# A two-layer macaron block on one core: the state of polynomial attention by 32x32 tiles instead of GpSimd passes, and another order of a unit's work on TensorE

## The chip, the cores and the metric

One core of one Trainium2 chip runs the whole program. The metric is device time in microseconds (us). Of the kernel before, three runs are shown; their median counts. Engines are named as in the profile: PE (TensorE; PEld its weight loads), DVE (VectorE), ACT (ScalarE), POOL (GpSimd), SP (SyncE, which issues the DMAs).

## The reference

Six sublayers follow each other on x of 4 x 1024 x 128 in float32: an MoE feed-forward, polynomial attention, the MoE again, a dense feed-forward, latent attention, the dense feed-forward again. The change touches the second one, `_L0_attn_ref`, with 16 heads of width 8:

```python
att = jnp.einsum('bhid,bhjd->bhij', q, k) * (1.0 / math.sqrt(hd))
att = jnp.where(causal[None, None], att, -jnp.inf)
lin = jnp.where((x >= -100) & (x <= 0), -0.01 * x + 1, 0.0)     # polymax(x) = (poly + lin) / 1000
poly = jnp.where(x > 0, x ** 2 + 1, 0.0)
y = jnp.einsum('bhij,bhjd->bhid', polymax(att), v)
return y.reshape(B, T, C) @ W_proj
```

## The kernel before

`attn0_phase` (from L888) works on one batch element after another. An element has 1024 tokens (8 tiles of 128) and 4 groups of 4 heads; one group of one element is a **turn** `m`, 16 in all. `pipeline` (L975) writes out the four turns of an element and loops over elements. In a turn the scores of 4 heads are made in 10 **units** k (`key_units`, L1500): for each half of the queries the diagonal tiles (units 0 and 3), two smaller units (1, 2 and 4, 5), and for the second half four full units of 128 keys by 512 queries (6 to 9). While turn m runs, the 10 **preparations** (`PREP`, L949) of turn m+1 are interleaved, one with each unit: keys k0, k1, four key/value pieces kv0 to kv3, queries q0, q1, and run0, run1.

A part of the function is linear in the score for all earlier keys, so the kernel keeps a running sum over key tiles of (key, value) products. run0 and run1 multiply keys by values on PE (L1063), DVE adds them up into `run` (L1333), and POOL makes the **state** from them by three passes over 128x1024 elements (`state`, L1003: mask and scale L1007, its low part L1011, the difference L1014). PE adds state times queries to the output (L1109), once for each half of the queries, right behind the products with `seen_one` (L1104).

Each engine runs its own queue in written order. On PE a turn is `step` (L1128): for every k the scores of unit k+1 (L1068), then preparation k (L1052, L1058 or L1063, all in the one PSUM bank `a_bank`), then for k >= 2 the values of unit k-2 (L1086), at k = 4 the small matmul `highest` (L1117) that tests the size of the scores. `values` ends a half with L1104 and L1109. ACT takes the rectified scores (L1229, or L1224 for the diagonal), then its part of the preparation (L1208 makes the low part of keys or queries, L1213 copies a kv piece), then squares (L1239), and copies the output at the end of a half (`copy_out`, L1243). DVE takes its half of the scores (`take`: L1365, or L1359 and L1361 for the diagonal), finishes keys and queries (L1315, L1320), the running sum, and the diagonal products (`diagonal`, L1372); the result of `highest` (L1348) it reads ahead of `take` of unit 6, `decide` follows at k = 6. POOL squares (L1021) and makes the state. A preparation waits until `a_bank` has been read by the one before it. At the end of a turn `correct` (L961) branches on the flag of that test; an element ends with the projection (L1182) and the residual sum.

Of the kernel before, what the change touches and what calls it, by code (L numbers as in the profile page):

```python
# [879 lines left out]
GW = 3 * P  # L880
# [7 lines left out]
def attn0_phase(nc, t, tag):  # L888


    with ExitStack() as ctx:
# [8 lines left out]
        first_rows = small[:, 3:4]  # L900
        state_mask, kv_ones, seen = small[:, 8:136], small[:, 136:392], small[:, 392:904]
        k_lift, minus_lift, half_lift = small[:, 904:905], small[:, 905:906], small[:, 906:907]
# [5 lines left out]
        KV = [sb(f"KV{q}", [P, BT, 2 * P]) for q in range(2)]  # L908
        run = sb("run", [P, BT, P])
        runm = sb("runm", [P, BT, P])  # L910
        runl = sb("runl", [P, BT, P], F32R)
        S = [sb(f"S{q}", [P, BT, P], F32R) for q in range(2)]
# [17 lines left out]
        runm_ready, runl_ready, S_ready = sem("runm_ready"), sem("runl_ready"), sem("S_ready")  # L930
# [21 lines left out]
        def width(u):  # L952

            pieces = units[u][1]
            return pieces[0][3] if len(pieces) == 1 else HALF

# [35 lines left out]
        with nc.Block() as block:  # L992
            @block.gpsimd
            def _(pool):
                for s in (runm_ready, runl_ready, S_ready, sq01_ready):
                    pool.sem_inc(s, LEAD)
                pool.memset(run[:, 0, :], 0.0).then_inc(zero_ready, 1)
                pool.wait_ge(w_in, 48)
                pool.tensor_scalar(seen_one[:, :], seen[:, 0:P], 1.0 + LIFT * LIFT, None, ALU.mult).then_inc(seen_set, 1)
                for q in range(2):  # L1000
                    pool.tensor_copy(KV[q][:, :, :], kv_ones.unsqueeze(1).to_broadcast([P, BT, 2 * P])).then_inc(kv_set, 1)

                def state(m, q):  # L1003

                    pool.wait_ge(av_ready, after(m * NU + NU - 1))
                    pool.wait_ge(y_ready, after((m - 1) * 2 - 1))
                    pool.tensor_tensor(runm[:, :, :], run[:, :, :], state_mask.unsqueeze(1).to_broadcast([P, BT, P]),  # L1007
                                       ALU.mult).then_inc(runm_ready, 1)
                    pool.wait_ge(runm_ready, after(m))
                    pool.sem_inc(pool_pause, 1)  # L1010
                    pool.tensor_tensor(runl[:, :, :], runm[:, :, :], k_low.unsqueeze(2).to_broadcast([P, BT, P]),  # L1011
                                       ALU.mult).then_inc(runl_ready, 1)
                    pool.wait_ge(runl_ready, after(m))
                    pool.tensor_tensor(S[q][:, :, :], runm[:, :, :], f32(runl[:, :, :]), ALU.subtract).then_inc(S_ready, 1)  # L1014

                def square(m, g, u):
                    n = width(u)
                    pool.wait_ge(read01, after(m * NU + u))
                    pool.sem_inc(pool_pause, 1)
                    r = R[:, slot(g % 2, u), 0:2, HALF - n:HALF]  # L1020
                    pool.tensor_tensor(r, r, r, ALU.mult).then_inc(sq01_ready, 1)  # L1021

                def step(m, g, b, more, has_next):
                    for u in OTHERS:
                        square(m, g, u)
                    if has_next:
                        state(m + 1, (g + 1) % 2)

                pipeline(pool, lambda: state(0, 0), step, lambda b, more: None)

            @block.tensor
            def _(pe):
# [3 lines left out]
                pe.wait_ge(w_low, 1)  # L1036
# [8 lines left out]
                def prepare(m, g, k):  # L1045
# [44 lines left out]
                def values(m, g, u):  # L1090
# [11 lines left out]
                    if end:  # L1102
# [25 lines left out]
                def step(m, g, b, more, has_next):  # L1128
                    for k in range(NU):
# [4 lines left out]
                        elif has_next:  # L1134
                            scores(m + 1, (g + 1) % GROUPS, 0)
                        if has_next:
# [4 lines left out]
                            if k == 5:  # L1141
# [32 lines left out]
                def finish(b, more):  # L1174
# [3 lines left out]
                    for s in range(2):  # L1178
                        for j in range(4):
                            for g in range(GROUPS):  # L1180
                                c = s * HALF + j * P
                                last = pe.matmul(e01[1][:, s, j * P:(j + 1) * P], yS[:, g, c:c + P], wp[:, g * DIM:(g + 1) * DIM],  # L1182
# [6 lines left out]
            def _(act):  # L1189
# [4 lines left out]
                act.activation(w[0][:, :, 0:P], w32[:, :, 0:P], ACT.Copy, scale=SCORE_SCALE)  # L1194
                act.activation(w[0][:, :, P:GW], w32[:, :, P:GW], ACT.Copy).then_inc(w_high, 1)
# [7 lines left out]
                def prepare(m, g, k):  # L1203
# [6 lines left out]
                    elif kind == "kv":  # L1210
                        act.wait_ge(ap_ready, after(m * NU + k))
                        act.wait_ge(y_ready, after((m - 1) * 2 - 1))
                        act.activation(KV[g % 2][:, 2 * i:2 * i + 2, :].rearrange("p j (g c) -> p (j g) c", c=ROW)[:, :, 0:3 * HD],  # L1213
                                       a_bank[:, :].rearrange("p (n c) -> p n c", c=ROW)[:, :, 0:3 * HD],
# [37 lines left out]
                def step(m, g, b, more, has_next):  # L1252
                    for k in range(NU):
                        if k + 1 < NU:
                            rectify(m, g, k + 1)
                        elif has_next:
                            rectify(m + 1, (g + 1) % GROUPS, 0)
                        if has_next:
# [5 lines left out]
                        if k == NQ0 + 1:  # L1264
                            copy_out(m, g, 0)
# [18 lines left out]
            def _(dve):  # L1284
# [5 lines left out]
                dve.wait_ge(w_high, 1)  # L1290
                dve.wait_ge(zero_ready, 1)
                dve.scalar_tensor_tensor(w[1][:, :, 0:P], w32[:, :, 0:P], SCORE_SCALE, f32(w[0][:, :, 0:P]), ALU.mult, ALU.subtract)
                dve.tensor_tensor(w[1][:, :, P:GW], w32[:, :, P:GW], f32(w[0][:, :, P:GW]), ALU.subtract).then_inc(w_low, 1)

# [13 lines left out]
                def prepare(m, g, k):  # L1308
# [13 lines left out]
                    elif kind == "run":  # L1322
                        dve.wait_ge(ap_ready, after(m * NU + k))
                        dve.wait_ge(runm_ready, after(m - 1))
                        last = 3 if i == 0 else 2
                        for h in range(last + 1):
# [6 lines left out]
                            ins = dve.tensor_tensor(run[:, c + 1, :], a_bank[:, h * P:(h + 1) * P], run[:, c, :], ALU.add)  # L1333
# [49 lines left out]
                def step(m, g, b, more, has_next):  # L1383
                    for k in range(NU):
                        if k == 5:
                            highest(m, g % 2)
# [4 lines left out]
                        if k == 6:  # L1391
# [45 lines left out]
A0_SMALL = 907  # L1437
SLOTS = 4


def attn0_weights(ctx, nc, t):

    t.attn0_w = ctx.enter_context(nc.sbuf_tensor("attn0_w", [P, GROUPS, GW], F32))
    t.attn0_wp = ctx.enter_context(nc.sbuf_tensor("attn0_wp", [P, GROUPS * DIM], F32))
# [21 lines left out]
def attn0_laid_out(np, a, r):  # L1466
    wqkv = a["L0_attn_W_attn"].reshape(DIM, 3, GROUPS, GH, HD)
    w = np.zeros((DIM, GROUPS, 3, GH, ROW), np.float32)
    for part in range(3):
        w[:, :, 0:2, :, part * HD:(part + 1) * HD] = wqkv[:, 0:2].transpose(0, 2, 1, 3, 4)  # L1470
    w[:, :, 2, :, 0:HD] = wqkv[:, 2]
    r["wqkv"] = w.reshape(P, GROUPS * GW)
    wp = np.zeros((GROUPS, GH, ROW, DIM), np.float32)
    wp[:, :, 0:HD] = a["L0_attn_W_proj"].reshape(GROUPS, GH, HD, DIM)
    r["wproj"] = wp.transpose(1, 2, 0, 3).reshape(P, GROUPS * DIM)
    row, col = np.arange(P) % ROW, np.arange(P)
    small = np.zeros((P, A0_SMALL), np.float32)
    small[:, 0] = ((row >= HD) & (row < 2 * HD)) | (row == 25)
    small[:, 1] = (row >= 2 * HD) & (row < 3 * HD)
    small[:, 2] = (row >= 24) & (row < 27)  # L1480
    small[row == 24, 904], small[row == 25, 904], small[row == 26, 904] = lift_parts(np)
    small[:, 905], small[:, 906] = -LIFT, HALF_LIFT
    small[:, 3] = row < HD
    small[:, 4:8] = np.arange(P)[:, None] // ROW == np.arange(GH)
    same = (np.arange(P)[:, None] // ROW) == (col[None, :] // ROW)
    small[:, 8:136] = same * np.where(row < 24, SLOPE, np.where(row < 26, 1.0 - HALF_LIFT * HALF_LIFT, 0.0))[:, None]
    small[:, 136:264] = ((row == 24) | (row == 25))[None, :]
    small[:, 392:904] = np.tile(np.triu(np.ones((P, P))), (1, 4))
# [699 lines left out]
```

## Time and profile before

| | us |
|---|---|
| median of 3 runs (3181.7 to 3197.34) | 3185.62 |
| the profiled execution | 3197.16 |
| its span, first to last instruction | 3195.4 |
| of it PE busy / DVE / ACT / POOL | 2832.2 / 2087.3 / 1199.9 / 836.7 |

The mean granted TensorE clock is 0.919 of full speed. The table is read with the stage in mind: these shares are averages over six sublayers with other limits, and the change touches one of them.

### The profile page before, as it was taken

Reading aid. Unit: us, or ns where it says so; the run is one execution under the profiler, and the core shown is the slowest. Engines: PE = TensorE matmul, PEld = TensorE weight load, DVE = VectorE, ACT = ScalarE, POOL = GpSimd, SP = SyncE. Lnnn points to the kernel's source line nnn. Section 1 sums busy time; section 2 is a strip of 40 time slices with the busy share of each in tenths; the row PEclk is TensorE's granted clock in tenths of the full one; section 3 lists DMA queues with packets and bytes.
Section 4 is the critical chain, followed back from the end, with each engine's and each line's share of the span. In section 5 each row is a group of like instructions: output and inputs, shape, how many; then the busy total and the mean of one; then the engine's idle time right before and its main releaser. Section 6 shows DMA issues by size and latency. Waiting matters only on the chain. (4 is left out here: it accounts for less than half of the span.)

```text
span 3195.4 us, 55424 instructions
## 1 busy us (share of the span) xinstructions
PE 2832.2 (89%) x15400; PEld 1924.1 (60%) x15400; DVE 2087.3 (65%) x5242; ACT 1199.9 (38%) x2164; POOL 836.7 (26%) x1220
## 2 busy tenths in 40 slices
PE   5999999958787888689999998869989989999986
PEld 4777777735555555467777776445465465465453
DVE  6777777747676777577777776355556556555533
ACT  2111111127565657521111111335545545545532
POOL 1222332225555555423222332001101101111100
PEclk8999999958888788899999998879999999999988
DMA  3000000000000000110000000000000000000000
GB/s 130 0 0 0 0 0 0 1 0 2 3 2 3 2 2 2 61 44 0 0 0 0 0 0 1 0 1 1 1 2 1 1 1 1 1 1 1 1 1 27
DMA packets 12996, 23.60 MB, mean 7 GB/s; under 512 B 2306, under 2 KB 7682, under 8 KB 12804
## 3 DMA queue, kind: packets, MB, share of 16 engines
q1 hardware_dynamic: 12804, 21.22, 2.0%
q8 instruction: 98, 1.61, 0.2%
q14 instruction: 94, 0.77, 0.1%
HBM read 18.52 MB, written 2.10 MB: 6 GB/s over the span
## 5 line engine op out<-in xcount | busy, mean ns | idle before, releaser
L555 DVE SCALAR_TENSOR_TENSOR moe_acc<-moe_ps,moe_comb,moe_acc 128x512 f32<-128x512 f32 x896 | 661.1, 744 | 174.5 <-PE moe_ps L304 167.9
L2017 DVE CUSTOM_DVE_ANT_0 attn_masked<-attn_psm,attn_causal 128x1024 f32<-128x1024 f32 (+7 forms) x512 | 367.6, 755 | 210.4 <-PE attn_psm L1742 199.3
L1921 ACT ACTIVATE attn_probs<-attn_pse 128x512 f32<-128x512 f32 (+1 forms) x640 | 319.9, 553 | 301.6 <-PE attn_pse L1756 301.0
L304 PE MATMUL moe_ps<-moe_Wg,moe_xh 128*128 128x512 f32 x1024 | 329.4, 403 | 25.0 <-DVE moe_Wu L501 25.0
L335 PE MATMUL moe_ps<-moe_Wd,moe_ih 128*128 128x512 f32 x1024 | 337.8, 411 | 0.0
L304 PE MATMUL moe_ps<-moe_Wu,moe_xh 128*128 128x512 f32 x1024 | 337.1, 411 | 0.0
L1772 PE MATMUL attn_psy<-attn_probs,attn_V 128*64 128x512 f32 (+3 forms) x1536 | 325.5, 524 | 0.3 <-POOL attn_probs L1677 0.3
L454 POOL TENSOR_SCALAR moe_part<-consts,moe_pick,moe_prob 128x8 f32<-128x8 f32 x256 | 98.1, 398 | 752.1 <-ACT moe_prob L389 752.1
L1677 POOL TENSOR_SCALAR_AFFINE_SELECT attn_probs<-attn_probs 128x256 f32<-128x256 f32 (+1 forms) x192 | 95.1, 495 | 757.7 <-ACT attn_probs L1921 757.7
L1021 POOL TENSOR_TENSOR attn_R<-attn_R 128x1024 f32<-128x1024 f32 (+1 forms) x128 | 215.5, 1690 | 201.6 <-DVE attn_R L1365 201.4
L1756 PE MATMUL attn_pse<-attn_qS,attn_kS 110*128 110x512 f32 (+3 forms) x768 | 233.2, 394 | 21.4 <-ACT attn_probs L1921 15.2
L304 PEld LDWEIGHTS moe_ps<-moe_Wg,moe_xh 128*128 128x128 f32 x1024 | 195.3, 192 | 73.9 <-issue 28.3
L1756 PEld LDWEIGHTS attn_pse<-attn_qS,attn_kS 110*128 110x128 f32 x768 | 120.0, 194 | 188.6 <-ACT attn_probs L1921 108.1
L388 ACT ACTIVATE moe_prob<-moe_gap 128x2 f32<-128x2 f32 x64 | 13.0, 203 | 548.4 <-DVE moe_gap L546 548.4
L335 PEld LDWEIGHTS moe_ps<-moe_Wd,moe_ih 128*128 128x128 f32 x1024 | 186.0, 191 | 41.8 <-issue 1.1
L304 PEld LDWEIGHTS moe_ps<-moe_Wu,moe_xh 128*128 128x128 f32 x1024 | 187.0, 192 | 36.7
L304 PE MATMUL moe_ps<-moe_Wg,moe_xl 128*128 128x512 f32 x512 | 204.6, 400 | 0.0
L304 PE MATMUL moe_ps<-moe_Wu,moe_xl 128*128 128x512 f32 x512 | 203.9, 398 | 0.0
L335 PE MATMUL moe_ps<-moe_Wd,moe_il 128*128 128x512 f32 x512 | 203.3, 397 | 0.0
L1742 PE MATMUL attn_psm<-attn_kS,attn_qS 108*128 108x512 f32 (+3 forms) x672 | 180.1, 374 | 18.6 <-DVE attn_mx L2017 18.3
L1365 DVE TENSOR_SCALAR attn_R<-attn_e 128x1024 f32<-128x1024 f32 (+1 forms) x128 | 138.7, 1084 | 53.4 <-PE attn_e L1068 47.2
L1086 PE MATMUL attn_y<-attn_R,attn_KV 128*32 128x128 f32 (+3 forms) x2304 | 170.8, 429 | 0.9 <-POOL attn_R L1021 0.8
(208 smaller groups left out, 4871.2 us busy)
## 6 DMA issues: line engine op xcount, KB each, us to landing
moe_stageg<-in_w_gate SPq DMA_DIRECT2D x8, 512.0 KB, 7.2
moe_stageu<-in_w_up SPq DMA_DIRECT2D x8, 512.0 KB, 8.3
moe_stageg<-in_w_down SPq DMA_DIRECT2D x8, 512.0 KB, 3.7
out<-X SPq DMA_DIRECT2D x1, 2048.0 KB, 8.9
attn_qS<-attn_mh SPq DMA_DIRECT2D x64, 4.0 KB
attn_qS<-attn_ml SPq DMA_DIRECT2D x64, 4.0 KB
attn_wd<-in_wd SPq DMA_DIRECT2D x1, 864.0 KB, 5.7
attn_w<-in_wqkv SPq DMA_DIRECT2D x1, 768.0 KB, 5.1
```

The source lines that it names most:

```text
L304: last = pe.matmul(expert_bank[j % 4][:, :], a[q][:, :], w[b][:, cols], start=k == 0, stop=k == 2)
L335: last = pe.matmul(y_bank[h][:, :], a[q][:, rows], W[2][b][:, cols], start=c == 0 and k == 0, stop=c == KC - 1 and k == 2)
L454: ins = pool.tensor_scalar(part[:, q, r, k, :], t.iota8, pick[:, q, r, k:k + 1], prob[:, q, r, k:k + 1], ALU.is_equal, ALU.mult)
L555: dve.scalar_tensor_tensor(acc[:, q, r, :], expert_bank[j % 4][:, :], comb[:, q, r, e:e + 1], acc[:, q, r, :], ALU.mult, ALU.add).then_inc ...
L1021: pool.tensor_tensor(r, r, r, ALU.mult).then_inc(sq01_ready, 1)
L1086: last = pe.matmul(y_bank[rows, qc:qc + n], KV[q][:, kt, P + j * ROW:P + (j + 1) * ROW], R[:, r, j, at_:at_ + n], start=first and k == 0, ...
L1365: dve.tensor_scalar(R[:, r, 0:2, HALF - n:HALF], e01[u % 2][:, :, HALF - n:HALF], LIFT, -HALF_LIFT, ALU.max, ALU.add).then_inc(read01, 1)
L1742: last = pe.matmul(m_all[:, base + lo:base + hi], qS[q][c][0:STACK, j * P:(j + 1) * P], keys[0:STACK, lo:hi], start=True, stop=True)
L1756: last = pe.matmul(e_bank[c][:, at_:at_ + n], kS[:, kt * P:(kt + 1) * P], qS[q][c][:, s * HALF + qc:s * HALF + qc + n], start=True, stop=True)
L1772: last = pe.matmul(y_bank[VW * c:VW * (c + 1), qc:qc + n], V[:, kt, :], probs[:, u % 2, c, at_:at_ + n], start=first and k == 0, stop=end, ...
L1921: act.activation(probs[:, u % 2, c, HALF - n:HALF], e_bank[c][:, HALF - n:HALF], ACT.Exp, scale=SCORE_SCALE).then_inc(p_ready, 1)
L2017: dve.tensor_tensor_reduce(masked[:, k % 2, 0:n], m_all[:, base:base + n], causal[:, SEQ - n:SEQ], 1.0, NEG, ALU.add, ALU.max, mx[:, q, v: ...
```

## The change

The weights of a group get a fourth part: keys twice, in the first 8 and second 8 of each head's 32 rows, already times -0.01, for the running sum alone. So `run` is the state as it stands, in full float32, one buffer for each parity of the group, and POOL's `state` is gone. PE multiplies the state by the queries as 32x32 tiles in full float32, four for a chunk of 128 queries, one per head. Each group has its own 8 of the 32 output rows of a head, so that the projection matrix is 128x128 instead of four of these. On PE the values of unit k-2 come ahead of preparation k; `highest` moves from k = 4 to k = 2, and on DVE its reading comes after `take` of unit 3, `decide` after `take` of unit 4; ACT copies the first half's output ahead of its part of preparation 4. The split weights are made in four pieces instead of two.

```diff
-                for s in (runm_ready, runl_ready, S_ready, sq01_ready):
...
+                pool.sem_inc(sq01_ready, LEAD)
+                for q in range(2):
+                    pool.memset(run[q][:, 0, :], 0.0).then_inc(zero_ready, 1)
...
-                def state(m, q):
...
-                    if has_next:
-                        state(m + 1, (g + 1) % 2)
...
-                pe.wait_ge(w_low, 1)
+                pe.wait_ge(w_low, 4)
...
-                                last = pe.matmul(a_bank[:, h * 2 * P:(h + 1) * 2 * P], xT[a][:, j * P:(j + 1) * P], w[b_][:, g, P:GW],
+                                last = pe.matmul(a_bank[:, h * 2 * P:(h + 1) * 2 * P], xT[a][:, j * P:(j + 1) * P], w[b_][:, g, 2 * P:GW],
...
+                    if end:
+                        pe.wait_ge(av_ready, after(m * NU + NU - 1))
...
-                        pe.wait_ge(S_ready, after(m))
                         chunks = [c for c in range(4 * s, 4 * s + 4) if c]
                         for c in chunks:
-                            last = pe.matmul(y_bank[:, (c % 4) * P:(c % 4 + 1) * P], S[q][:, c, :], qS[q][:, c * P:(c + 1) * P],
-                                             start=False, stop=c == chunks[-1], skip_group_check=True)
+                            for j in range(GH):
+                                rows = slice(j * ROW, (j + 1) * ROW)
+                                last = pe.matmul(y_bank[rows, (c % 4) * P:(c % 4 + 1) * P], run[q][rows, c, rows],
+                                                 f32(qS[q][rows, c * P:(c + 1) * P]), start=False, stop=c == chunks[-1],
+                                                 skip_group_check=True)
...
                 def highest(m, g, has_next):
                     if has_next:
-                        pe.wait_ge(av_ready, after((m + 1) * NU + 4))
+                        pe.wait_ge(av_ready, after((m + 1) * NU + 1))
...
+                        if k >= 2:
+                            values(m, g, k - 2)
+                        if k == 2:
+                            highest(m, g, has_next)
                         if has_next:
...
-                            if k == 5:
+                            if k == 2:
                                 pe.wait_ge(top_ready, after(m))
                             prepare(m + 1, (g + 1) % GROUPS, k)
                         if opens(g, more, k):
                             pe.wait_ge(av_ready, after((m + 1) * NU + k))
                             open_half(b + 1, k - (NU - 2))
-                        if k >= 2:
-                            values(m, g, k - 2)
-                        if k == 4:
-                            highest(m, g, has_next)
...
-                act.activation(w[0][:, :, 0:P], w32[:, :, 0:P], ACT.Copy, scale=SCORE_SCALE)
-                act.activation(w[0][:, :, P:GW], w32[:, :, P:GW], ACT.Copy).then_inc(w_high, 1)
+                for k, factor in enumerate(FACTORS):
+                    act.activation(w[0][:, :, k * P:(k + 1) * P], w32[:, :, k * P:(k + 1) * P], ACT.Copy,
+                                   scale=factor).then_inc(w_high, 1)
...
+                        if k == NQ0 + 1:
+                            copy_out(m, g, 0)
                         if has_next:
                             prepare(m + 1, (g + 1) % GROUPS, k)
                         if opens(g, more, k):
                             high_x(b + 1, k - (NU - 2))
                         if k + 1 < NU:
                             square(m, g, k + 1)
-                        if k == NQ0 + 1:
-                            copy_out(m, g, 0)
...
-                        dve.wait_ge(runm_ready, after(m - 1))
+                        dve.wait_ge(y_ready, after((m - 1) * 2 - 1))
...
-                            ins = dve.tensor_tensor(run[:, c + 1, :], a_bank[:, h * P:(h + 1) * P], run[:, c, :], ALU.add)
+                            ins = dve.tensor_tensor(run[q][:, c + 1, :], a_bank[:, h * P:(h + 1) * P], run[q][:, c, :], ALU.add)
...
-                        if k == 5:
-                            highest(m, g % 2)
                         if k + 1 < NU:
                             take(m, g, k + 1)
                         elif has_next:
                             take(m + 1, (g + 1) % GROUPS, 0)
-                        if k == 6:
+                        if k == 2:
+                            highest(m, g % 2)
+                        if k == 3:
                             decide(m, g % 2)
```

## Rows read from the trace of the kernel before

**Rows 1.** Windows view, the turns of polynomial attention: us, busy us by engine (instructions), granted clock.

```profile
core 0: us, PE busy (x) PEld busy (x) DVE busy (x) ACT busy (x) POOL busy (x), PEclk, DMA share, GB/s
710.00:1338.00 628.00, 510.89 (x4870) 329.25 (x4870) 458.75 (x604) 399.86 (x478) 345.53 (x175) 0.83 0.01 3
```

**Rows 2.** Windows view, the second turn of the second element in four stretches.

```profile
909.70:911.00 1.30, 0.00 (x0) 0.00 (x0) 1.30 (x2) 0.60 (x1) 1.30 (x1) 1.00 0.03 6
911.00:912.50 1.50, 1.40 (x11) 0.82 (x11) 1.50 (x1) 0.79 (x1) 1.32 (x2) 1.00 0.07 16
912.50:922.40 9.90, 7.45 (x69) 5.33 (x69) 7.80 (x9) 6.49 (x9) 7.57 (x4) 0.50 0.01 2
922.40:943.80 21.40, 20.31 (x215) 12.21 (x211) 16.39 (x24) 17.03 (x20) 11.42 (x7) 0.99 0.01 2
```

**Rows 3.** Timeline at that turn's beginning: start, us, engine, line, [idle before, releaser].

```profile
908.59 4.51 DVE L1372 SCALAR_TENSOR_TENSOR attn_R<-attn_R,attn_T 128x1024 f32<-128x1024 f32 x2
908.72 3.31 POOL L1007 TENSOR_TENSOR attn_runm<-attn_run,attn_small 128x1024 f32<-128x1024 f32 x1 [3.72 <-DVE attn_run L1333]
...
909.02 0.64 PE L1109 MATMUL attn_y<-attn_qS,attn_S 128*128 128x128 f32 x4
...
911.05 0.51 PE L1068 MATMUL attn_e<-attn_qS,attn_kS 32*128 32x384 f32 x8 [1.39 <-issue]
...
912.72 0.68 ACT L1208 ACTIVATE attn_low<-attn_a,attn_small 128x512 fp32r<-128x512 f32 x1
...
914.16 0.73 DVE L1315 SCALAR_TENSOR_TENSOR attn_kS<-attn_a,attn_small,attn_low 128x512 fp32r<-128x512 f32 x1
...
914.95 1.65 PE L1052 MATMUL attn_a<-attn_xT,attn_w 128*128 128x512 f32 x3 [1.39 <-DVE attn_kS L1315]
...
920.61 2.37 DVE L1372 SCALAR_TENSOR_TENSOR attn_R<-attn_R,attn_T 128x1024 f32<-128x1024 f32 x2 [0.16 <-ACT attn_R L1224]
```

**Rows 4.** Lines view by shape, stage of polynomial attention: diagonal products, and POOL's first state pass.

```profile
L1372 DVE SCALAR_TENSOR_TENSOR attn_R<-attn_R,attn_T 128x1024 f32<-128x1024 f32 x64 | 111.2, 1779 | 2.8 <-ACT attn_R L1224 2.8
...
L1007 POOL TENSOR_TENSOR attn_runm<-attn_run,attn_small 128x1024 f32<-128x1024 f32 x16 | 49.6, 3098 | 98.4 <-DVE attn_run L1333 98.4
```

**Rows 5.** Timeline of PE, preparations that wait: into group 2's turn, in the very first turn.

```profile
947.09 1.64 PE L1052 MATMUL attn_a<-attn_xT,attn_w 128*128 128x512 f32 x3 [2.07 <-issue]
...
718.27 1.65 PE L1052 MATMUL attn_a<-attn_xT,attn_w 128*128 128x512 f32 x3 [5.32 <-DVE attn_kS L1315]
```

**Rows 6.** Timeline of PE, late in the turn of rows 2: preparations 7 and run0, values.

```profile
929.08 1.08 PE L1086 MATMUL attn_y<-attn_R,attn_KV 128*32 128x128 f32 x32
...
933.36 0.96 PE L1052 MATMUL attn_a<-attn_xT,attn_w 128*128 128x512 f32 x3 [0.42 <-DVE attn_qS L1320]
...
935.98 1.16 PE L1063 MATMUL attn_a<-attn_KV 128*128 128x128 f32 x8 [0.66 <-DVE attn_qS L1320]
```

**Rows 7.** Timeline of PE, the turn that opens an element: the second half's transposes.

```profile
981.13 1.11 PE L1042 MATMUL attn_a<-consts,attn_xn 128*128 128x128 f32 x4 [2.51 <-DVE attn_run L1333]
```

**Rows 8.** Timeline, middle of the turn of rows 2, k = 4 and 5.

```profile
926.25 1.16 PE L1104 MATMUL attn_y<-attn_seen_one,attn_KV 128*128 128x128 f32 x8
...
927.16 0.53 PE L1109 MATMUL attn_y<-attn_qS,attn_S 128*128 128x128 f32 x3
...
928.18 0.77 PEld L1058 LDWEIGHTS attn_a<-attn_w,attn_xT 128*128 128x128 f32 x6 [0.24 <-DVE attn_peak L1348]
...
928.40 1.11 ACT L1229 ACTIVATE attn_R<-attn_e,attn_small 128x1024 f32<-128x1024 f32 x1
```

**Rows 9.** Timeline of the same turn, k = 2 and 3.

```profile
916.53 1.12 PE L1068 MATMUL attn_e<-attn_qS,attn_kS 32*128 32x128 f32 x16
...
918.10 1.21 DVE L1359 TENSOR_TENSOR attn_T<-attn_e,attn_small 128x1024 f32<-128x1024 f32 x1
...
918.24 1.65 PE L1058 MATMUL attn_a<-attn_w,attn_xT 128*128 128x256 f32 x6 [0.59 <-DVE attn_kS L1315]
...
919.82 1.94 PE L1086 MATMUL attn_y<-attn_R,attn_KV 128*32 128x128 f32 x32
921.69 0.80 PE L1068 MATMUL attn_e<-attn_qS,attn_kS 32*128 32x384 f32 x8
```

**Rows 10.** Timeline, start of the stage: DVE splits the weights; page, the weights' DMA.

```profile
670.98 1.35 DVE L1292 SCALAR_TENSOR_TENSOR attn_w<-attn_w 128x512 fp32r<-128x512 f32 x1 [1.91 <-ACT attn_w L1195]
...
attn_w<-in_wqkv SPq DMA_DIRECT2D x1, 768.0 KB, 5.1
```

More of the change, by code:

```diff
@@ L877, in ffn_laid_out @@
     r["ffn_small"] = small
-GW = 3 * P
+GW = 4 * P
 ROW = 32
@@ L907, in attn0_phase @@
         qS = [sb(f"qS{q}", [P, SEQ], F32R) for q in range(2)]
[L908 to L912, printed above, removed]
+        KV = [sb(f"KV{q}", [P, BT, 2 * (P + q * WINDOW)]) for q in range(2)]
+        run = [sb(f"run{q}", [P, BT, P]) for q in range(2)]
         R = sb("R", [P, SLOTS, GH, HALF])
@@ L955, in width, with parts @@
             return pieces[0][3] if len(pieces) == 1 else HALF
+        def parts(q, j):
+            half = P + q * WINDOW
+            both = KV[q][:, j:j + 2, :].rearrange("p j (a n) -> p (j a) n", n=half)
+            return both[:, :, 0:P].rearrange("p a (n c) -> p a n c", c=ROW)[:, :, :, 0:WINDOW]
         def slot(q, u):
@@ L1000, in _ @@
                 for q in range(2):
-                    pool.tensor_copy(KV[q][:, :, :], kv_ones.unsqueeze(1).to_broadcast([P, BT, 2 * P])).then_inc(kv_set, 1)
-                def state(m, q):
[L1005 to L1014, printed above, removed]
+                    pool.memset(KV[q][:, :, P:], 0.0)
+                    pool.tensor_copy(KV[q][:, :, 0:P], k_ones.unsqueeze(1).to_broadcast([P, BT, P])).then_inc(kv_set, 1)
                 def square(m, g, u):
@@ L1025, in step @@
                         square(m, g, u)
-                    if has_next:
-                        state(m + 1, (g + 1) % 2)
-                pipeline(pool, lambda: state(0, 0), step, lambda b, more: None)
+                pipeline(pool, lambda: None, step, lambda b, more: None)
             @block.tensor
@@ L1179, in finish @@
                         for j in range(4):
+                            c = s * HALF + j * P
                             for g in range(GROUPS):
-                                c = s * HALF + j * P
-                                last = pe.matmul(e01[1][:, s, j * P:(j + 1) * P], yS[:, g, c:c + P], wp[:, g * DIM:(g + 1) * DIM],
+                                last = pe.matmul(e01[1][:, s, j * P:(j + 1) * P], yS[:, g, c:c + P], wp[:, :],
                                                  start=g == 0, stop=g == GROUPS - 1)
@@ L1289, in _ @@
                 res.prime(dve)
[L1290 to L1293, printed above, removed]
+                dve.wait_ge(zero_ready, 2)
+                for k, factor in enumerate(FACTORS):
+                    part = slice(k * P, (k + 1) * P)
+                    dve.wait_ge(w_high, k + 1)
+                    dve.scalar_tensor_tensor(w[1][:, :, part], w32[:, :, part], factor, f32(w[0][:, :, part]),
+                                             ALU.mult, ALU.subtract).then_inc(w_low, 1)
                 def normalise(b):
@@ L1466, in attn0_laid_out @@
 def attn0_laid_out(np, a, r):
-    wqkv = a["L0_attn_W_attn"].reshape(DIM, 3, GROUPS, GH, HD)
-    w = np.zeros((DIM, GROUPS, 3, GH, ROW), np.float32)
+    wqkv = a["L0_attn_W_attn"].reshape(DIM, 3, GROUPS, GH, HD).transpose(1, 0, 2, 3, 4)
+    w = np.zeros((DIM, GROUPS, 4, GH, ROW), np.float32)
     for part in range(3):
-        w[:, :, 0:2, :, part * HD:(part + 1) * HD] = wqkv[:, 0:2].transpose(0, 2, 1, 3, 4)
-    w[:, :, 2, :, 0:HD] = wqkv[:, 2]
+        rows = slice(part * HD, (part + 1) * HD)
+        w[:, :, 0, :, rows], w[:, :, 1, :, rows] = wqkv[0], wqkv[1]
+        if part < 2:
+            w[:, :, 2, :, rows] = wqkv[1]
@@ L1472, in attn0_laid_out @@
+    wp = np.zeros((GH, ROW, DIM), np.float32)
+    for g in range(GROUPS):
+        w[:, g, 3, :, V_FROM[g]:V_FROM[g] + HD] = wqkv[2][:, g]
+        wp[:, V_TO[g]:V_TO[g] + HD] = a["L0_attn_W_proj"].reshape(GROUPS, GH, HD, DIM)[g]
     r["wqkv"] = w.reshape(P, GROUPS * GW)
[L1473 to L1476, printed above, removed]
+    r["wproj"] = wp.reshape(P, DIM)
@@ L1484, in attn0_laid_out @@
     small[:, 4:8] = np.arange(P)[:, None] // ROW == np.arange(GH)
[L1485 to L1488, printed above, removed]
+    small[row == 24, 8], small[row == 25, 8], small[row == 26, 8] = lift_parts(np)
+    small[:, 9], small[:, 10] = -LIFT, HALF_LIFT
@@ L1489, in attn0_laid_out @@
+    small[:, 12:12 + P] = np.where(row == 24, 1.0 - HALF_LIFT * HALF_LIFT, 0.0)[None, :]
+    small[:, 12 + P:] = np.tile(np.triu(np.ones((P, P))), (1, 4))
     r["attn0_small"] = small
```

26 lines of the change are left out of this document (12 added, 14 removed).

## The prediction

> **What bounds the kernel now.** I read the windows first. The turns of polynomial attention take 628 of 3195.4 us, PE is busy for 510.89 of them, and its granted clock is 0.83 [rows 1]; nothing outside this stage changes. Then one ordinary turn, cut where the clock changes [rows 2]: 34.1 us, of them 29.2 with PE busy (0 + 1.40 + 7.45 + 20.31). PE stands idle for 1.30 at the start; from 912.5 to 922.4 it runs at 0.50, the 1.2 GHz level, with gaps; afterwards it is nearly full at 2.4 GHz. So PE's queue sets the turn, with about 5 us of gaps and a slow stretch behind the first of them. Last the timeline of the turn's beginning, to see who makes the gaps [rows 3]. DVE's two diagonal products take 4.51 there and 2.37 later in the turn; in the first case POOL's mask pass runs beside them. Over the stage they cost 111.2 us, where 64 at 2.37 / 2 would be 75.8: 35.4 us go to POOL's company [rows 4]. The PE queue sees that only through the keys: preparation 1 waits 1.39 for them at 914.95 [rows 3].
>
> **The change, part by part.** Delays in this part come from a schedule that I wrote by hand for that turn from the durations and releases of the timeline; I give the step that each rests on.
>
> *POOL's three passes go.* That is 2.14 us less on DVE at each turn's start (4.51 - 2.37). The products then end at 910.96 instead of 913.10. But `take` of unit 1 needs scores that PE starts at 911.05, so it ends near 913.0, and the keys need ACT's low part, ready at 912.72 + 0.68 = 913.40 [rows 3]. They start at 913.45 instead of 914.16: 0.7 of the 2.14 is on the path. That holds for the turns of groups 1 and 3, 8 in all: -5.6. Into group 2 PE reaches preparation 0 only at 947.09, after an issue wait of 2.07, so nothing is won; into a new element PE waits for the projection. The first turn waits 5.32 at preparation 1, where 1.39 is usual [rows 3, 5]: -3.9. Sum **-9.5**. Bounds: 0 and -35.4.
>
> *Values ahead of preparations.* Late in a turn preparation 7 waits 0.42 and run0 0.66 for DVE's queries [rows 6]; values now fill that. ACT has hardly a gap there, so units do not come faster, but the tail of values is shorter: by my schedule PE's last values end 0.45 sooner in 15 turns, **-6.8**; bounds 0 and 15 x 1.08 = -16. In the 3 turns that open an element PE stands 2.51 at the second transposes with values queued behind them [rows 7]; one unit of values now runs before that: 3 x 1.2, **-3.6**; bounds 0 and -7.5.
>
> *State by 32x32 tiles.* 7 matmuls of a turn become 28, in full float32, two records each. The nearest row of the same count is 32 records of 128 columns on 128x32 tiles, 1.08 us [rows 6]; I take that for the second half (4 x 4 tiles) instead of 0.64 [rows 3], and three quarters, 0.83, for the first instead of 0.53 [rows 8]. Before, L1109 starts 0.25 ahead of the end of L1104 (926.25 + 1.16 against 927.16 [rows 8]); with another tile shape behind L1104 I count this overlap as lost. So the end of the turn is 0.44 + 0.25 = 0.7 later: 16 x 0.7 = **+11.2**. Bounds: 0 below (the products alone are no shorter than now), and above the price of tiles that run one after another, in the rivals.
>
> *The turn at k = 4.* Preparation 4 now stands behind values, L1104 and the state, about 2.3 us. Behind it are ACT's kv copy, a square, and the rectification of unit 6, which began at 928.40 [rows 8]; in my schedule it begins at 929.1, the state's own 0.55 included: 15 x 0.7 = **+10.5**. Bounds 0 and 15 x 1.6.
>
> *`highest` at k = 2.* The wait of 0.24 ahead of preparation 5 goes [rows 8]: 15 x 0.24 = **-3.6**. In its place PE waits at preparation 2 until DVE has done unit 3's two masks (1.21 each) and the reading. From scores at 916.1 (before 916.53), values to 919.05 and `highest` to 919.25, PE waits until about 920.15, and the scores of unit 4 start at 921.75, against 921.69 [rows 9]: **0**, because the same two masks held the scores of unit 4 anyway.  Behind that wait are queued preparation 2 and ACT's kv copies, and through them everything of k = 3. On DVE the reading waits for nothing, as `highest` is done before the masks are; unit 3's diagonal products stand a little later behind it. The new wait for run1 at the end of a half is long satisfied, as the old one for POOL was.
>
> *The rest.* ACT's and DVE's split weights come in four pieces: at most two more of 1.35 on DVE [rows 10], before PE's first matmul, once: **+1.5**, between 0 and +2.7. The weights' DMA (768 KB, 5.1 us to land) grows by a third and the projection's shrinks; both are issued some hundred us ahead under the first MoE stage; without that cover it would be a few us. The kv copy writes 256 elements for 384; it ends no wait here.
>
> Sum: -9.5 - 6.8 - 3.6 + 11.2 + 10.5 - 3.6 + 1.5 = -0.3 us, on the profiled execution's 3197.16. Against the median of 3185.62, which lies 11.5 lower, that is **3185**, no change. A measurement of this kernel can tell about 0.5% (16 us, the spread of its three runs) from none. The bounds of these terms, not all at one end, span 3170 to 3201.
>
> **The rivals.**
>
> *Tiles one after another (slower).* The four state tiles of a chunk read different rows and write one bank. The trace shows row tiles side by side only for scores that go to four banks (L1068, 8 matmuls of 384 columns in 0.51 [rows 3]), and tiles in one bank side by side only by columns (L1086 [rows 6]). If a state tile has to wait for the one before it, a record costs as in L1104, 0.91 / 8 = 0.114 from its start to that of L1109 [rows 8]: 32 and 24 records take 3.65 and 2.74 instead of 1.08 and 0.83, 4.5 a turn, all on PE's path: +72, **3257**. For it: no row has this case. Against it: the four tiles write different partitions of that bank. It decides from the first turn. The Trainium skill, TensorEngine Tiling (Array Packing), Gotcha 1: PSUM Pressure, says that different row tiles cannot use one PSUM bank at the same time; by that rule the sum is the 3257 above, and no run here shows it yet. Chance 0.16.
>
> *The clock comes back later (slower).* The new wait of 0.9 at preparation 2 cuts PE's work just where the clock is at 1.2 GHz. Before, the only gap there was 0.59, and the clock rose at 922.4, after PE had been busy without a gap since 918.24 [rows 2, 9]. If it rises as much later as PE's unbroken work begins later (920.15 for 918.24), near 924.3, then values of unit 1 and preparation 3 run at half speed: about 1.5 a turn, 15 x 1.5 = +22, **3207** (3202 to 3213). Against it: ahead of the wait PE is busy from 914.2 to 919.25, so the clock may as well rise earlier. Chance 0.14.
>
> *DVE's start decides (faster).* If my schedule puts too much on ACT's low part, the whole 2.14 counts in 15 turns (-36 with the first turn, instead of -9.5), and the delay at k = 4 (+10.5) disappears in the time won: 3185 - 26 - 10.5, **3148** (3135 to 3169). For it: keys and masks at k = 0 to 3 hang on DVE. Against it: the group 2 turns, whose start waits on issue [rows 5]. Chance 0.27.
>
> *The change does not free DVE.* POOL's squares could fall beside the diagonal products as its passes did. Before, they do not where the products take 2.37, and they move with `take`, so I leave this within the forecast (its time would be 3194).
>
> **How the numbers follow.** No change 0.43 (3170 to 3201), the faster rival 0.27, the two slower ones 0.16 and 0.14. The range 3138 to 3225 takes in the forecast, nearly all of the faster case, and the clock case with the spread of the runs; it leaves out the serial tiles and a little on the fast side, just under 2 in 10. Faster by over 0.5%: 0.27, within 0.43, slower 0.30.
>
> **What would show it.** Right: L1372 alike at both places of a turn (near 75.8 us in all), no POOL work but squares, the state's matmuls at about 1.1 and 0.85 us, an ordinary turn near 34 us, kv copies later at k = 4. Wrong: state matmuls of 3 us or more; a clock of 0.50 that lasts much longer or shorter than 9.9 us a turn; or turns of 32 us, with PE waiting less at preparation 1.

## The result, and the profile after

The kernel after takes 3231.14 us (median of 4 runs, 3228.03 to 3237.42) where the kernel before takes 3185.95 beside it: a ratio of 1.013, 95% interval 1.011 to 1.0149. It is 45 us **slower**, outside the range of the prediction, and none of its rivals is the reason.

The windows view of the stage in the profiled execution (3230.05 us, span 3228.3), with the columns of [rows 1]:

```profile
709.00:1377.00 668.00, 523.83 (x5654) 335.90 (x5650) 421.26 (x604) 394.28 (x477) 214.61 (x128) 0.85 0.01 3
```

Against [rows 1] the stage is 40 us longer, though DVE is busy for 37.5 us less and POOL for 130.9 less. PE is busy for 12.9 more and stands idle for 144.2 instead of 117.1 (the windows' length less PE's busy time). What was to change did, as the lines view by shape says:

```profile
L1365 DVE SCALAR_TENSOR_TENSOR attn_R<-attn_R,attn_T 128x1024 f32<-128x1024 f32 x64 | 75.5, 1221 | 1.8 <-ACT attn_R L1215 0.2
...
L1099 PE MATMUL attn_y<-attn_qS,attn_run 32*32 32x128 f32 x896 | 30.9, 271 | 0.0
```

The diagonal products cost 75.5 us for the 111.2 of [rows 4]. The state's tiles cost 30.9 where its products (L1109) took 18.8 before; these 12.1 are nearly all that PE is busy longer. The rest of the loss is in PE's waits, here of the stage before (the waits view: who waited <- for whom: us in all, times, longest):

```profile
PE attn_e L1068 <- issue: 20.2, 13, 2.2
...
PE attn_a L1052 <- issue: 6.6, 3, 2.4
...
PE attn_e L1182 <- issue: 5.7, 3, 2.1
```

and of the stage after:

```profile
PE attn_e L1055 <- issue: 51.1, 13, 4.4
PE attn_a L1039 <- DVE attn_kS L1308: 23.8, 15, 4.1
PE attn_e L1173 <- issue: 17.6, 4, 4.7
PE attn_a L1045 <- DVE attn_peak L1341: 16.4, 15, 1.3
```

Issue, the time in which PE waits for nothing that the profile shows, goes from 32.5 to 68.7 us. After, all of it but one wait of 2.1 stands behind the branch of `correct`, ahead of the first matmuls of the next turn or of the projection. Before, 22.0 of it stands there; the rest is five waits at other places, three of them ahead of preparation 0 (6.6 us, the 2.07 of [rows 5] among them). Call the idle time of the array between the last matmul ahead of the branch and the first one behind it the **gap**: the 16 gaps add up to 24.5 us before and 66.6 after, 2.6 a turn more. The timeline of PE at the end of the turn of [rows 2, 3], before:

```profile
905.39 2.78 PE L1086 MATMUL attn_y<-attn_R,attn_KV 128*32 128x512 f32 x24
908.11 1.16 PE L1104 MATMUL attn_y<-attn_seen_one,attn_KV 128*128 128x128 f32 x8
```

L1109 follows at 909.02 and the next scores at 911.05 [rows 3]. One turn's end after:

```profile
950.75 1.16 PE L1093 MATMUL attn_y<-attn_seen_one,attn_KV 128*128 128x128 f32 x8
951.84 1.08 PE L1099 MATMUL attn_y<-attn_qS,attn_run 32*32 32x128 f32 x32
956.97 0.80 PE L1055 MATMUL attn_e<-attn_qS,attn_kS 32*128 32x384 f32 x8 [4.06 <-issue]
```

PE's sequencer has records of its own: the view by source line shows the branch itself (PEldq is PE's sequencer; ns min/median/max, start). The branch ahead of 911.05 in the kernel before:

```profile
L967 PEldq COMPARE_BRANCH  x1: 3270/3270/3270, 907.3 to 907.3; - x1
```

the one ahead of 956.97 in the kernel after, and all 16 of it:

```profile
L968 PEldq COMPARE_BRANCH  x1: 3522/3522/3522, 952.9 to 952.9; - x1
...
L968 PEldq COMPARE_BRANCH  x16: 3327/3640/3932, 744.3 to 1363.7; - x16
L968 DVEq COMPARE_BRANCH  x16: 56/56/74, 744.5 to 1357.9; - x16
L968 ACTq COMPARE_BRANCH  x16: 45/45/54, 745.1 to 1364.4; - x16
```

The branch took 3.3 us before as well (all 16: 1.90 to 3.81, median 3.46). But there it began at 907.3, and the array had work until 909.66: 2.36 of the branch was covered, and 1.39 of idle time was left. After, it begins at 952.9 and the array ends at 952.92: nothing is covered, and the gap is 4.06.

### The profile page after: what moved, and what is told of

The parts are those of the page before. It is cut to its first block and busy times, and to the rows that moved or that the text cites. A ratio compares the mean times of both kernels' runs of the same rounds, so it can differ in the third digit from the quotient of the medians.

```text
span 3228.3 us, 56907 instructions
## 1 busy us (share of the span) xinstructions
PE 2836.9 (88%) x16184; PEld 1927.6 (60%) x16184; DVE 2050.2 (64%) x5244; ACT 1194.6 (37%) x2166; POOL 703.9 (22%) x1175
```

## The experiments

Q, F, O and T stand for theories in the expectations. Q: a queue of instructions ahead of the branch. F: first the length of the program, later the fetch of what lies behind the jump. O: the order of the turn. T: the small tiles themselves. "Branch" is PE's record at the branch (min/median/max, us), stage and PE busy are from the windows view, from the first scores to the end of the last projection.

| kernel | us | ratio (95%) | branch | stage | PE busy, clock |
|---|---|---|---|---|---|
| before | 3186 to 3194 | 1 | 1.90/3.46/3.81 | 628 | 510.9, 0.83 |
| after | 3231.1 | 1.013 (1.011, 1.0149) | 3.33/3.64/3.93 | 668 | 523.8, 0.85 |
| state early | 3165.3 | 0.9918 (0.9902, 0.9935) | 3.41/3.63/3.85 | 601 | 503.0, 0.89 |
| state wide | 3218.6 | one run | 3.28/3.51/3.74 | 657 | 531.5, 0.83 |
| old order | 3238.4 | 1.0145 (1.0128, 1.0162) | 3.31/3.62/3.93 | 675 | 533.1, 0.83 |
| 16 records less | 3220.8 | one run | 0.44/3.49/3.91 | 660 | 522.8, 0.84 |
| after, short body | 3170.1 | 0.9948 (0.9932, 0.9965) | 0.20/0.23/0.36 | 605 | 504.3, 0.89 |
| before, short body | 3173.9 | 0.9955 (0.994, 0.9971) | 0.20/0.22/0.33 | 607 | 493.7, 0.86 |
| early, short body | 3142.0 | 0.9852 (0.9818, 0.9885) | 0.20/0.22/0.35 | 579 | 493.2, 0.91 |
| order alone | 3181.8 | 0.9981 (0.9958, 1.0004) | 1.66/3.49/3.86 | 635 | 511.1, 0.83 |
| one unit earlier | 3217.0 | 1.0082 (1.0056, 1.0109) | 3.30/3.65/5.21 | 656 | 530.0, 0.84 |
| early, old order | 3197.0 | 1.0027 (1.0014, 1.004) | 3.29/3.65/4.96 | 631 | 517.0, 0.87 |

### The state's tiles early

The tiles stand behind the first values of each half instead of the last; the products with `seen_one` end a half.

```diff
-                    if end:
+                    if first:
                         pe.wait_ge(av_ready, after(m * NU + NU - 1))
...
+                    if first:
+                        chunks = [c for c in range(4 * s, 4 * s + 4) if c]
...
+                    if end:
+                        for n_, (kt, at_, qc, n, _) in enumerate(key_units(s)[0]):
```

> PE's wait ahead of the first scores of a turn (issue) was 1.39 in the ordinary turn before and is about 4.0 after. Theory Q (queue): PE needs about 5.1 us from the branch at the end of a turn to the next matmul, and starts on it only when no more than some 64 instructions (32 matmuls and 32 weight loads) are still to run; the 32 small state matmuls last 1.08, so 4.0 show. With the state's tiles moved behind the first values of each half and L1093 last, the 64 instructions are 8 records of L1093 and 24 of values, some 3.9 us: the wait falls to about 1.2, the time by 16 x 2.8 = 45, to about 3186 or a little less. Theory F (length of the program): the turn has as many PE instructions as before the move, so the wait stays at 4 and the time near 3231. Theory O (the order of values and preparations makes the wait): the same, 3231.

3165.29 us, 66 below the kernel after and **faster than both kernels**. The gap falls, so O and F as the length of the program are out; Q has the direction, with 1.2 expected for the gap and 2.09 measured. The timeline of PE at a turn's end:

```profile
924.84 1.92 PE L1073 MATMUL attn_y<-attn_R,attn_KV 128*32 128x512 f32 x16
926.69 1.16 PE L1101 MATMUL attn_y<-attn_seen_one,attn_KV 128*128 128x128 f32 x8
929.95 0.50 PE L1055 MATMUL attn_e<-attn_qS,attn_kS 32*128 32x384 f32 x8 [2.09 <-issue]
```

and the branch ahead of 929.95:

```profile
L968 PEldq COMPARE_BRANCH  x1: 3717/3717/3717, 925.8 to 925.8; - x1
```

The branch is no shorter, but it begins 2.05 us before the array runs out (926.69 + 1.16 = 927.85). PE's waits in the stage:

```profile
PE attn_e L1055 <- issue: 25.9, 13, 2.2
...
PE attn_a L1045 <- DVE attn_peak L1342: 4.2, 15, 0.5
PE attn_a L1039 <- DVE attn_qS L1314: 3.6, 15, 0.3
PE attn_e L1174 <- issue: 2.7, 1, 2.7
```

Issue falls from 68.7 to 28.6 (-40.1) and the wait for DVE's reading at preparation 2 from 16.4 to 4.2 (-12.2), because the first half's tiles now run where PE waited for it. PE is busy for 20.8 less with the same work, at a granted clock of 0.89 for 0.85. The windows view of the gap, here and in the kernel after:

```profile
927.85:929.95 2.10, 0.01 (x3) 0.04 (x2) 2.10 (x4) 0.96 (x2) 0.00 (x0) 1.00 0.02 4
...
952.92:956.97 4.05, 0.00 (x0) 0.03 (x1) 1.43 (x2) 0.60 (x1) 0.00 (x0) 0.75 0.03 6
```

Here the clock stays at 2.4 GHz over the gap, and the first scores take 0.50; behind 4.06 they take 0.80. It does fall here too, a little later: the windows give 0.50 from 932 to 935 and 1.00 again from 938, in the kernel after 0.50 from 956.97 to 963 and 1.00 again from 966.

### The state in one matmul a chunk

One 128x128 float32 matmul stands for the four tiles; it mixes the heads, so the separation of heads in the state's share of the output is left out.

```diff
-                            for j in range(GH):
...
+                            last = pe.matmul(y_bank[:, (c % 4) * P:(c % 4 + 1) * P], run[q][:, c, :],
+                                             f32(qS[q][:, c * P:(c + 1) * P]), start=False, stop=c == chunks[-1],
...
```

> One 128x128 matmul per chunk in place of four 32x32 tiles, at the same place; it mixes the heads, so the state's part of the output is left out of the function computed. 7 float32 matmuls (14 records) a turn instead of 56 records. Q: the last 64 instructions then last about 3.8 us, the wait is near 1.3, the time near 3188. F: the program is 84 PE instructions a turn shorter, the wait falls as well. O: wait 4, time 3231.

3218.62 us, the gap 2.5 to 3.2 in every turn: it falls, as Q and F had it, by half of what Q gave. The second half's state takes 1.06, as the tiles do, in 8 records instead of 32. The branch begins in the middle of the products ahead of it, at 948.6, and so 1.2 of it is covered (948.73 + 1.06 = 949.79):

```profile
947.74 1.16 PE L1093 MATMUL attn_y<-attn_seen_one,attn_KV 128*128 128x128 f32 x8
948.73 1.06 PE L1097 MATMUL attn_y<-attn_qS,attn_run 128*128 128x128 f32 x8
952.55 0.72 PE L1055 MATMUL attn_e<-attn_qS,attn_kS 32*128 32x384 f32 x8 [2.77 <-issue]
```

### The new state in the old order

The kernel after with the order of before in `step` of PE, ACT and DVE.

```diff
-                        if k >= 2:
-                            values(m, g, k - 2)
-                        if k == 2:
-                            highest(m, g, has_next)
                         if has_next:
...
+                        if k >= 2:
+                            values(m, g, k - 2)
+                        if k == 4:
+                            highest(m, g, has_next)
```

> The changed state with the old order of a turn (preparation before values, highest at k = 4, the copies as before). Q and F: the end of the turn is the same stretch of small matmuls, the wait stays near 4, the time near 3231 (3220 to 3240). O: the wait is back at 1.4, the time near 3186.

3238.43 us, with gaps of 3.8 to 4.5: the order is not what costs the time. O falls.

### Sixteen records less at the end

The state of chunks 4 and 5 is left out of the second half's output.

```diff
-                        chunks = [c for c in range(4 * s, 4 * s + 4) if c]
+                        chunks = [c for c in range(4 * s, 4 * s + 4) if c and c not in (4, 5)]
```

> Only the chunks 6 and 7 of the second half get their state (16 records instead of 32 at the end of a turn); the state's part for the chunks 4 and 5 is left out. Q: the last 64 instructions are 16 state records (0.54), 8 of L1093 (0.9) and 8 of values (1.0), 2.4 us: the wait is about 2.6, the time about 3207. F: 32 PE instructions a turn of some 450 fewer, the wait about 3.8, the time about 3222. O: wait 4.

3220.81 us. Both theories missed it: the gap is about 1.1 to 1.3 at 4 of the turn ends and 3.9 to 4.7 at the others, though what stands before the branch is the same. Two of them on the timeline of PE:

```profile
915.92 0.64 PE L1099 MATMUL attn_y<-attn_qS,attn_run 32*32 32x128 f32 x16
917.65 0.51 PE L1055 MATMUL attn_e<-attn_qS,attn_kS 32*128 32x384 f32 x8 [1.09 <-issue]
...
950.26 0.64 PE L1099 MATMUL attn_y<-attn_qS,attn_run 32*32 32x128 f32 x16
954.92 0.80 PE L1055 MATMUL attn_e<-attn_qS,attn_kS 32*128 32x384 f32 x8 [4.02 <-issue]
```

PE's sequencer shows the difference. The branch ahead of 917.65 took 0.436 us:

```profile
L968 PEldq COMPARE_BRANCH  x1: 436/436/436, 916.8 to 916.8; - x1
```

In the loop it is the branch between groups 0 and 1 that is short, each time; in the last element, which is written out behind the loop, it is the one between groups 1 and 2. So the place in the program decides, not the work. The DMA view gives the reason: it lists packets of instructions. In the 4 us of the long branch of the kernel after (953.0 to 957.0) one of 16 KB arrives (q8), and one of 8 KB (q14):

```profile
q8 instruction: 1, 0.02, 1.8%
q14 instruction: 1, 0.01, 0.7%
```

and during the short branch here (916.5 to 917.6) none:

```profile
DMA packets 0, 0.00 MB, mean 0 GB/s; under 512 B 0, under 2 KB 0, under 8 KB 0
```

That made a new theory F: the branch jumps over PE's whole correction (144 matmuls) to instructions that are not there yet, and waits until they are fetched. The other branches bear it out. In the kernel after, one 16 KB packet starts 0.9 to 1.5 us into each of the 16. In the kernel before, the three short ones of 1.90 to 2.50 us are those whose packet was started between 0.4 us ahead of the branch and 0.1 behind its beginning. All four short ones here have none; the 8 KB packets come with some of the long ones only.

### The jumped body made short, in three kernels

TensorE's part of the correction for small arguments is left out, which these inputs never enter; its two counts stay. One edit in the kernel after, in the kernel before, and in the kernel with the state early:

```diff
-                    correct(pe, pe_pause, m, g % 2, lambda: low_scores(m, g), ((cs_ready, US), (cv_ready, NU)))
+                    correct(pe, pe_pause, m, g % 2, lambda: [pe.sem_inc(cs_ready, US), pe.sem_inc(cv_ready, NU)],
+                            ((cs_ready, US), (cv_ready, NU)))
```

> The kernel after, with TensorE's copy of the correction (the body that the branch at a turn's end jumps over, which these inputs never enter) replaced by its two semaphore counts; the work that is done is unchanged. Theory F (the branch itself takes 3.3 to 3.9 us on TensorE's sequencer because it jumps over 144 matmuls to instructions that must first be fetched; what stands before it only decides how much of that shows): the branch's record falls to about 0.44 us, its fastest in the run with 16 records left out, the idle time before a turn's first scores from about 4.1 to about 1.0 us, and the time by 16 x 3.1 = 50 us, from 3231 to about 3181. Theory Q (the sequencer waits at the branch until the queued matmuls have run, whatever is jumped over): gap 4.1 us still, time 3231. Theory T (the small tiles cost this time themselves): 3231 too.

> The kernel before, with TensorE's copy of the correction replaced in the same way. F: the branch's record falls from 2.5 to 3.8 us to about 0.4, the gap of 1.4 to 2.1 us at a turn's end goes to nearly nothing, since 16 matmuls are still queued at the branch: 16 x 1.6 = 26 us less, about 3160. Q and T: 3186, unchanged.

> The kernel with the state's tiles moved ahead of the branch by whole units (3165 us), and TensorE's copy of the correction replaced in the same way. F: the gap of 2.0 to 2.2 us goes to nearly nothing: 16 x 2.05 = 33 us less, about 3132, and 45 to 50 us below the kernel after with the short body, since there the flag's load still shows (about 1.0 us a turn) and the order of the state's tiles keeps its other gains. Q: 3165, unchanged. T: the same 66 us below the kernel after with the short body as without it.

3170.10, 3173.87 and 3142.03 us. The branches of the kernel after with the short body:

```profile
L968 PEldq COMPARE_BRANCH  x16: 200/232/359, 743.7 to 1304.8; - x16
```

and one turn's end of it, with the tiles last as in the kernel after:

```profile
933.55 1.08 PE L1099 MATMUL attn_y<-attn_qS,attn_run 32*32 32x128 f32 x32
935.41 0.50 PE L1055 MATMUL attn_e<-attn_qS,attn_kS 32*128 32x384 f32 x8 [0.79 <-issue]
```

F holds, Q as the cause of the gap and T fall: nothing was changed in what runs, and the gap goes from 4.06 to 0.79, the 16 gaps from 66.6 to 14.0. The 16 KB packets in the stage go from 79 to 51, after and after with the short body:

```profile
q8 instruction: 79, 1.29, 0.8%
...
q8 instruction: 51, 0.84, 0.5%
```

None of the 51 starts during a branch. The kernel after gains 61 us (50 expected). PE is also busy for 19.6 less with the same work, at a clock of 0.89 for 0.85, and other waits take a part of this back. The kernel before gains only 0.45% or 14 us (26 expected). There the gap goes to nothing, but PE then waits longer for the keys and for ACT:

```profile
PE attn_a L1052 <- DVE attn_kS L1316: 39.0, 15, 5.3
PE attn_e L1068 <- ACT attn_R L1230: 18.8, 17, 1.8
```

(28.0 and 8.7 us before). So what the branch costs is 1.8% of the kernel after (1.013 for 0.9948, 58 us) and 0.45% of the kernel before, 14 us. The difference, 44 us, is the whole result. **With the branch short in both, the change is worth 0.9948 for 0.9955, nothing that can be measured.** With the state early the short body is worth 23 us, not the 33 expected; ACT is late next there too (PE waits 29.1 for it, 16.8 with the long body).

### The order alone, on the old state

> The kernel before with only the new order of a unit's turn (scores, values, preparation, and the bound's chain at unit 2); GpSimd still builds the masked state. If the order is worth on the old state what it is worth on the new one (3238 to 3231): about 3179. If it is worth only what was forecast for the opening turns and the bound's chain: -6.8 - 3.6 - 3.6 = -14, about 3172. If the values now wait for GpSimd's passes: 3190 or more. The gap at the branch should stay at 1.4 to 2.1 us, since the last matmuls before it are the old ones.

The edit is the reverse of the one on the old order, in the kernel before. 3181.77 us, but its ten runs spread from 3169.74 to 3200.47: 0.9981, between 0.9958 and 1.0004, so between -13 and +1 us. It fits the first case, and doesn't prove a gain. The profiled execution is the slowest of the ten, so its stage in the table is not typical. The gap did not stay as expected everywhere: at six turn ends it is gone, because enough matmuls were still queued at the branch, at 824 for instance 3.44 us of values, which cover a branch of 3.29 in full.

### The tiles one unit earlier, and the early tiles in the old order

The first moves the tiles behind the values of the last unit but one of each half; the second is the early kernel with the order of before.

```diff
-                    if first:
+                    if u in (NQ0 - 2, NU - 2):
```

> The kernel after, with the state's tiles moved by one unit only: they stand behind the values of the last unit but one of each half, so that the last unit's values and the eight seen products are what TensorE has queued at the branch. Theory F (the branch takes 3.3 to 3.9 us whatever stands before it, and only long matmuls queued behind it hide some): branch records of 3.3 to 3.9 us as in the kernel after, but an idle time of 2.0 to 2.2 us before the next scores, as where the tiles were moved by whole units; that is worth 16 x 2.0 = 32 us, so 3199. If all of the 66 us of the kernel with the tiles moved early come from the branch and the clock that follows from it: 3165. If the tiles had to leave the turn's end altogether: gap 3.8 to 4.6 us still and 3231.

> The kernel with the state's tiles moved early (3165 us), with the order of before in a unit's turn (scores, preparation, values, and the bound's chain at units 4 to 6). If the new order is worth here what it is worth with the tiles last (3238 to 3231): about 3172. If the order matters only where the branch is shown in full: 3165. If, as forecast for the kernel before, the order is worth 14 us: about 3179. The gap at the branch should stay near 2.1 us, since the same values and seen products stand last.

3217.03 and 3197.02 us: both expectations missed. One unit earlier the gap is 2.4 to 3.2 at most turn ends, not 2.1: the sequencer comes to the branch only as the products with `seen_one` begin, and 1.1 to 1.3 is covered. At two turn ends, and at five of the other kernel, the branch itself takes 4.2 to 5.2:

```profile
L968 PEldq COMPARE_BRANCH  x1: 4997/4997/4997, 908.9 to 908.9; - x1
```

During all of these but the one of 4.2, two 16 KB packets start instead of one.

The first gains 14 us of the early kernel's 66, though issue is 20 us shorter. The rest of the 66 needs the early place: the tiles in DVE's shadow (the wait at preparation 2 is 16.3 here, as in the kernel after, against 4.2), and the clock of 0.89 for 0.84. In the old order the early tiles have no such shadow: their kernel is 32 us slower than in the new order, where 5 to 7 was the order's worth with the tiles last. How those 32 us divide between waits, branch and clock stays open.

## Why the prediction was wrong

**The step that failed** is the price of the state's tiles at the turn's end, "So the end of the turn is 0.44 + 0.25 = 0.7 later: 16 x 0.7 = +11.2". The tiles themselves were sized rightly: 1.08 us for 32 records as forecast, 0.86 for 24 (0.83 forecast), side by side though they write one bank. They add 12.1 us in all. What was taken over unpriced is the issue wait behind them, 1.39 in [rows 3]. It is the uncovered end of a branch of 3.3 us. The rest of that branch ran behind matmuls that were already queued when it began, 2.36 us of values, `seen_one` and L1109; with the tiles last the sequencer comes to the branch only as the array runs out, and this cover is gone. (The 2.07 of [rows 5] is another wait: it stands behind the next turn's first scores, after a branch of 2.48 and a gap of 0.72, and a 16 KB packet arrives in it, at 944.79. It is gone after.) The bound "the products alone are no shorter than now" looks at the array alone. In the traces the gaps grow by 42 us (24.5 to 66.6), where the term had 11.2; issue as a whole grows by less, 36.2, because some 8 us of waits at other places go, which the prediction did not have. With the cover made irrelevant (short bodies) the loss is gone, and what is left comes to about 0, as the sum did. That does not confirm the single terms, several of which missed:

- **POOL's passes go** (-9.5): DVE's part came as priced (75.5 us, 75.8 forecast). PE's wait for the keys fell from 28.0 to 23.8 only, the first turn's from 5.3 to 4.1, not to 1.39: 4.2 of the 9.5.
- **Values ahead of preparations** (-6.8, -3.6): the 9.8 us of waits at run0 and run1 are gone, but the second transposes, 11.2 us in 6 waits before [rows 7], still wait for 11.1. The terms of the order together, k = 4 and `highest` in them, were -3.5; the runs show -6 (-13 to +1) on the old state and -7 on the new one by the medians, whose intervals overlap.
- **The turn at k = 4** (+10.5): PE's waits for ACT's rectification grow from 8.7 to 14.1 over the stage; how much of that stands at k = 4 was not separated.
- **`highest` at k = 2** (-3.6 and 0): the -3.6 rests on a misread line. The 0.24 of [rows 8] is idle time of PE's weight loads (PEld), beside which PE's matmuls show none; PE itself waited for that reading in three turns, 4.4 us. The new wait at preparation 2 is 1.1 a turn, 0.9 forecast. It is 16.4 us where 13.1 (4.4 for the reading, 8.7 for the keys) stood in the same preparations before: a few us dearer than nothing.
- **Tiles one after another** (3257): refuted, 896 records take 30.9 us. The rule of the Trainium skill that was weighed there, TensorEngine Tiling (Array Packing), Gotcha 1, does not hold for these four tiles, which read different rows and write different partitions of one bank.
- **The clock comes back later** (3207): not as told. The stage's clock is 0.85 for 0.83, and in the turn shown it is back at 1.00 by 966, about 10 us after it fell in the gap, as in [rows 2] (9.9). That a shorter branch raises it, to 0.89, the short body shows; why it falls where it does stays open.
- **DVE's start decides** (3148): refuted; DVE's 37.5 us are free, PE's wait for the keys falls by 4.2, and with short branches the change still wins nothing that can be measured.

The Trainium skill has the mechanism, which the prediction passed over: Runtime: NRT & Kernel Launch, Instruction fetch mechanics, says that a taken branch to a target outside the resident instructions forces a fetch before execution goes on. The traces agree: 16 KB packets, and 3.3 to 3.9 us for the long jump against 0.20 to 0.36 for the short one. The price that the Trainium skill, Advanced Engine Details and Errata, Control Flow Timing, gives for a compare-and-branch, about 108 ns, holds for neither.

That the sequencer comes to the branch earlier where long matmuls stand last is shown by the branch's start in the kernels: 2.36 us before the array ran out in the kernel before, 2.05 with the tiles early, 1.2 with the wide state, 1.1 to 1.3 with the tiles one unit earlier, 0 in the kernel after. Why it is that late with the tiles, whether its queue counts instructions, was only argued: Q's figures failed in three runs (state early, state wide, 16 records less).

## What to carry to other kernels

An "issue" wait that recurs at one place is the uncovered end of something: look up the sequencer's records of the lines just ahead of it, price that thing in full, and ask of every edit there what still covers it. Ahead of a branch put long matmuls, not many short ones that run side by side; where a branch guards a large body that is hardly ever run, skipping the body can cost a fetch each time. Here the change costs 45 us with the tiles at the turn's end and gains 26 (0.9918) with the tiles where PE waited anyway.

## What the runs showed of the hardware

- A conditional branch on PE that jumps over 144 matmuls mostly takes 3.3 to 3.9 us, with a 16 KB packet of instructions that starts about 1 us into it. It takes 1.7 to 2.5 where the packet started before the branch or just as it began, up to 5.2 where two come, and 0.44 where none does. Over two counts it takes 0.20 to 0.36. At the same line DVE's takes 56 to 74 ns and ACT's 45 to 54, over bodies of their own.
- Four 32x32 float32 tiles on the diagonal of the array, writing one PSUM bank, run side by side: 32 records in 1.08 us.
- Over a gap of 2.09 us the granted clock stayed at 2.4 GHz (the next scores took 0.50), and was at 0.50 by 932, 2 us behind it; over one of 4.06 it was 0.75, and the same scores took 0.80.
